# Transposing a feed-forward weight into SBUF in two parts, half of it into a buffer of its own, ahead of the end of attention

## The reference

```
x = hidden_states                       # (4, 4096, 1024) f32
# attention block
h = layernorm(x);  q, k, v = h@Wq+bq, h@Wk+bk, h@Wv+bv      # 8 heads of 128
scores = einsum('bngh,bmgh->bnmg', q, k) / 32
probs  = softmax(scores, axis=-1)       # over the 8 HEADS, for each pair of tokens
x = x + einsum('bnmg,bmgh->bngh', probs, v)
# feed-forward block
h = layernorm(x);  prev = h shifted by one token (zeros first)
xr = mu_r*h + (1-mu_r)*prev;  xk = mu_k*h + (1-mu_k)*prev
x = x + sigmoid(xr @ W_r.T) * (square(relu(xk @ W_k.T)) @ W_v.T)
```

## Time and profile before

| | us |
|---|---|
| timed runs | 1914.25 and 1846.76, median 1880.5 |
| profiled execution, whole | 1842.97 |
| its span, slowest core (core 2) | 1841.4 |
| spans of the 8 cores | 1832.2 to 1841.4 |
| TensorE, VectorE, ScalarE busy on core 2 | 1202.3, 1161.5, 949.2 |
| attention ends, last products L576 on core 2 | about 1565 |
| feed-forward, first L797 to the end of the span | 1590.05 to 1841.4 |

### The profile page before, as it was taken

One profiled execution on the slowest core, in us unless ns is written; L12 is line 12 of the kernel. 1 busy time (PEld: TensorE's weight loads), 2 busy tenths in 40 slices (PEclk: granted clock), 3 DMA queues, 4 the chain that ended last, 5 costly groups with the idle time before them and its releaser, 6 DMA issues.

```text
span 1841.4 us, 33138 instructions; the slowest of 8 cores (1832.2 to 1841.4 us)
## 1 busy us (share of the span) xinstructions
PE 1202.3 (65%) x9912; PEld 837.1 (45%) x9912; DVE 1161.5 (63%) x1864; ACT 949.2 (52%) x1216; POOL 107.2 (6%) x136
## 2 busy tenths in 40 slices
PE   1676278888884556556555665665655566468898
PEld 1443134444342555444544545454554555335554
DVE  1655022222221887888888888888888887657875
ACT  0333022222222787787878878788787866112121
POOL 1002000000000000000000000000000000000000
PEclk6676689999997998999999999899999977689999
DMA  9027933333315465464545546446454555531011
GB/s 232 5 29 89 133 42 76 76 75 76 76 59 161 123 177 148 141 190 137 155 150 165 155 141 191 140 141 176 153 155 139 169 191 170 92 69 47 24 47 58
DMA packets 157112, 219.57 MB, mean 119 GB/s; under 512 B 54032, under 2 KB 127888, under 8 KB 154704
## 3 DMA queue, kind: packets, MB, share of 16 engines
q1 hardware_dynamic: 108624, 120.98, 24.2%
q0 software_dynamic: 48320, 96.48, 21.0%
HBM read 197.51 MB, written 36.44 MB: 127 GB/s over the span
## 4 chain that ended last, share of the span: by engine, by line
PE 33%; ACT 23%; DVE 22%; DMA 10%; issue 8%; SPq 1%; DVEq 1%; ACTq 1%; POOL 0%; POOLq 0%
ACT arena L500 20%; PE stAB L226 14%; PE stAB L480 11%; DMA vtspill<-scratch 6%; DVE arena L548 5%; DVE scratch L513 3%; PE ctxP L264 2%; DMA x_res<-x 2%; DVE scratch L518 2%; DVE scratch_f L521 2%; PE stAB L797 2%; DMA arena<-qspill 1%; PE stAB L836 1%; PE ctxP L203 1%; PE stAB L857 1%
## 5 line engine op out<-in xcount | busy, mean ns | idle before, releaser
L500 ACT ACTIVATE arena<-stAB 128x2048 bf16<-128x2048 f32 (+1 forms) x288 | 513.3, 1782 | 102.2 <-PE stAB L480 94.8
L480 PE MATMUL stAB<-arena 128*128 128x256 bf16 (+1 forms) x2304 | 312.1, 282 | 372.9 <-ACT arena L500 354.8
L480 PEld LDWEIGHTS stAB<-arena 128*128 128x128 bf16 x2304 | 206.6, 102 | 449.4 <-issue 419.7
L548 DVE TENSOR_TENSOR arena<-arena,scratch 128x2048 bf16<-128x2048 bf16 (+1 forms) x288 | 335.8, 1166 | 32.8 <-PE ctxP L576 2.1
L576 PE MATMUL ctxP<-arena 128*128 128x128 bf16 x4352 | 316.1, 229 | 31.7 <-DVE arena L548 23.3
L226 PE MATMUL stAB<-arena,wa 128*128 128x512 bf16 (+1 forms) x1344 | 321.6, 398 | 11.9 <-ACT arena L337 11.9
L576 PEld LDWEIGHTS ctxP<-arena 128*128 128x128 bf16 x4352 | 285.8, 103 | 53.8 <-issue 47.5
L513 DVE TENSOR_TENSOR scratch<-arena 128x1024 bf16<-128x1024 bf16 (+1 forms) x288 | 190.8, 663 | 85.2 <-ACT arena L500 68.7
L226 PEld LDWEIGHTS stAB<-arena,wa 128*128 128x128 bf16 x1344 | 136.4, 103 | 173.3 <-issue 51.9
L253 DVE TENSOR_SCALAR scratch<-scratch,cvecsb 128x512 bf16<-128x512 bf16 (+1 forms) x104 | 36.6, 352 | 253.5 <-ACT scratch L249 253.5
L249 ACT ACTIVATE scratch<-stAB 128x512 bf16<-128x512 f32 (+1 forms) x104 | 59.2, 572 | 252.5 <-PE stAB L226 183.3
(11 more groups left out here) (60 smaller groups left out, 785.9 us busy)
## 6 DMA issues: line engine op xcount, KB each, us to landing
arena<-kspill SPq DMA_DIRECT2D x72, 1024.0 KB, 9.2
arena<-vtspill POOLq DMA_DIRECT2D x72, 1024.0 KB, 10.6
x_res<-x SPq DMA_DIRECT2D x1, 8704.0 KB, 35.3
kspill<-scratch SPq DMA_DIRECT2D x8, 1024.0 KB, 5.3
vtspill<-scratch SPq DMA_DIRECT2D x8, 1024.0 KB, 9.2
out<-x_res SPq DMA_DIRECT2D x8, 1024.0 KB, 4.1
qspill<-scratch SPq DMA_DIRECT2D x8, 544.0 KB, 2.8
arena<-qspill POOLq DMA_DIRECT2D x8, 512.0 KB, 12.3
```

The source lines that it names most:

```text
L480: r = e.matmul(stAB[:, g * w:(g + 1) * w], arena_ap(KQ0 + par_k * 4096 + g * 512 + mcq * 128, [[1, 128]]), arena_ap(qbase2 + g * w, [[1, w]]),
L500: return e.activation(arena_ap(EA0 + par_e * 2048, [[1, NH * w]]), stAB[:, 0:NH * w], AF.Exp, scale=1.0 / 32.0)
L548: lambda e, w=w, par_u=par_u, par_e=par_e, par_d=par_d: e.tensor_tensor(arena_ap(UB0 + par_u * 2048, [[1, NH * w]]), arena_ap(EA0 + par_e ...
```

## The change

W_k's eight transposes leave the loop of 24. Four of them (`cj` 4 to 7) go to a new SBUF buffer `wkbuf` (4096 bfloat16 columns, 8 KB on each partition) and wait only for `d_ws0`; in SP's order they stand behind attention's last k load. The other four (`cj` 0 to 3) go where they went before, columns 8192 to 12287, which is the v buffer of the even quads, and wait for the products of step 283 (`m_ctx[NIT - 5]`), the last that reads that buffer. The order of `cj` in the queue becomes 4, 5, 6, 7, 0, 1, 2, 3. The sixteen transposes of W_r and W_v keep gates and order. The L797 matmuls read `cj` 4 to 7 from `wkbuf`; their number and order stay.

```diff
     ctxs = sbuf("ctxs", 2048, F32)
+    wkbuf = sbuf("wkbuf", 4096, BF16)
     wa = sbuf("wa", 6144, BF16)
@@
-    for wi, gate in [(1, None), (0, ("t_ffn", 1)), (2, ("t_ffn", 9))]:
+    for cj in range(4, NC):
+        ev("sync", [("d_ws0", 16 * 12)], "d_tw",
+           lambda e, cj=cj: e.dma_start_transpose(
+               bass.AP(wkbuf, (cj - 4) * 1024, [[wkbuf.shape[1], 128], [1, 1024]]),
+               bass.AP(wspill, 8 * 128 * D + cj * 128, [[D, 1024], [1, 128]])), 16)
+    for cj in range(4):
+        ev("sync", [("t_ctx", m_ctx[NIT - 5]), ("d_ws0", 16 * 12)], "d_tw",
+           lambda e, cj=cj: e.dma_start_transpose(
+               arena_ap(8192 + cj * 1024, [[1, 1024]]),
+               bass.AP(wspill, 8 * 128 * D + cj * 128, [[D, 1024], [1, 128]])), 16)
+    for wi, gate in [(0, ("t_ffn", 1)), (2, ("t_ffn", 9))]:
         for cj in range(NC):
             gw = [("t_ctx", total_ctx), ("v_du", total_du), ("t_st", total_st),
-                  ("d_ws0", 16 * 12)]
-            if gate is not None:
-                gw.append(gate)
+                  ("d_ws0", 16 * 12), gate]
@@ op_k
-                    r = e.matmul(ps[:, 0:wch],
-                                 arena_ap((8 + cj) * 1024 + dj * 128, [[1, 128]]),
+                    if cj < 4:
+                        wsrc2 = arena_ap((8 + cj) * 1024 + dj * 128, [[1, 128]])
+                    else:
+                        wsrc2 = bass.AP(wkbuf, (cj - 4) * 1024 + dj * 128,
+                                        [[wkbuf.shape[1], 128], [1, 128]])
+                    r = e.matmul(ps[:, 0:wch], wsrc2,
```

## The result

The changed kernel took 1.0054 of the time of the kernel before (95% interval 1.004 to 1.0067): 10.0 us more on 1846.3. Its median over 13 runs was 1858.56 us (1852.82 to 1927.89), that of the kernel before over the 10 runs beside it 1846.27 us (1842.44 to 1914.25). That is inside the 2% and inside the range of 1835 to 1885, but it is a slowdown clear of the interval, and the forecast was 0.2 us.

The account below looks back on a forecast made before the run. Attention was read as bound by ScalarE's exponential, the stretch to L836 by gate `t_ffn` >= 1 and SP's issue. Terms 0 + 0.2 = +0.2 us gave 1843.2; half way to 1846.76 + 0.2 gave 1845, range 1835 to 1885.

Parts of the forecast that it names:

- Term: 0, because none was there: After attention, 1565 to 1580: moving W_k's transposes away removes no wait, since W_k already landed 9.2 us before use.
- The gates of W_r and W_v keep their waits: Feed-forward: SP reaches the gates about 12 us earlier; L836 and L857 still wait 7.0 and 12.5 us; term 0.
- The order on SP and in time: End of attention: four transposes issue behind the last k load, 1540.6 to about 1546.6; the other four from about 1559.0.
- V of quad 6 lands 1.25 us later: End of attention, step 280: v lands at 1551.45 beside the transposes, 0.2 us past its reader.
- a factor of 1.33: Slowdown assumed for v beside the transposes, from v beside the k load, 8.9 us, against v alone, 6.7.
- quad 7 "Term: 0": Last v load, read at step 284: at most 1.2 us of slowing against 2.3 us to spare, so no cost.
- The slack of 1.0 us: Step 280: v of quad 6 landed at 1550.2 and its first reader ran at 1551.21.
- The bound of 5.9 us, and 2 more for quad 7: End of attention: most that quad 6's v is delayed if served behind all four transposes, plus 2 us for quad 7's.
- If the engines take turns by packet ... 0.4 us.: Argument against a late v: its 280 packets let only about 280 short transpose packets pass, 0.4 us.
- The slower rival: Attention's tail, product of step 280, waits for v: up to 6.9 us, 1850; chance 0.2.
- The faster rivals: Feed-forward starts when W_k is there, gain 0, or W_r issues sooner, at most 7.0 us, 1836; chance 0.05.

Follow-up runs that it names:

- x5_own_sems: Kernel before, W_k, W_r and W_v each on their own semaphore and the t_ffn gates removed: 0.9883 of the kernel before.
- x3_plain256: Changed kernel with the four early transposes replaced by plain DMAs of the same bytes in 256-byte pieces: 1.0024 of the kernel before.
- x4_one_early: Changed kernel with one of the four wkbuf transposes early and the other three behind attention's end: 1.0041 of the kernel before.
- x2_after_v: Changed kernel with the four early transposes also waiting until quad 7's v load has landed: 1.0006 of the kernel before.
- p1_probe: Changed kernel, its early transposes replaced by one transpose per quad of slices 2 to 5, in four positions: spans 1896 to 1923 us, before some 1840.
- y3_iso_sp: Kernel before plus an unread 1 MB load from SP, ahead of W_k's eight transposes at attention's end: load landed in 6.6 to 8.5 us.
- y2_iso_pool: Kernel before plus an unread 1 MB load from GpSimd beside W_k's eight transposes at attention's end: load landed in 7.2 to 8.4 us.

## Why the prediction was right in part and wrong in its number

- *"Term: 0, because none was there", for W_k's leaving the stretch from 1565 to 1580.* Right: from attention's end to the end of the span it is 277.0 us after, 277.3 before; in the changed kernel's core 2 the first L811 waited 12.85 us for the mix, as before.
- *The gates of W_r and W_v keep their waits.* Right: 5.9 and 11.1 us. x5_own_sems shows that this was where the time lay.
- *The order on SP and in time.* The distances between k, the first transpose and v are right to 0.1 us (0.6 and 0.6 against 0.6 and 0.7). The length of the issue is not: 24.75 us for four, not 6, so that the other four began at 1565.29 and not at 1559.0. That cost nothing, as W_k still landed over 20 us before L811.
- *V of quad 6 lands 1.25 us later, "a factor of 1.33", quad 7 "Term: 0".* This is the step that failed. V of quad 6 landed 10.8 us later on core 2 (19.7 against 8.9), v of quad 7 14.8 us later (21.5 against 6.7), and the L577 products waited 10.6 to 19.1 us over the eight cores (median 13.2) in place of 0 to 1.8. The place was right, the size was short by a factor of about nine. The slack of 1.0 us was right for core 2 alone: on five of the eight cores the kernel before already waited for v there. I took the price of a neighbour from k beside v, two plain loads, as it was the only pair in the trace. x3_plain256, the plain form of the same bytes, came out between (12.6 us); the transposing form did not.
- *The bound of 5.9 us, and 2 more for quad 7.* Wrong as a bound. It added up packet times measured alone: four transposes at 5.9 us of all engines. In company their packets took about 79 ns in the mean where they took 22 alone, as some stood for up to 3.3 us. A bound of this sort holds only if the cost of a packet stays what it was.
- *"If the engines take turns by packet ... 0.4 us."* Refuted by x4_one_early: one transpose, about 1056 packets, held v up by as much as 11 us.
- *The slower rival*, chance 0.2, 1850: the right mechanism in the right place, under-priced. Its sign, a wait for v of over 1 us near the end, is what came. It gave 6.9 us at the most where 10 were lost. By the rule of the Trainium skill that I set beside the row (DMA: Bandwidth & Descriptors, Issuing engines are not separate DMA queues), the DMAs interleave; the runs agree so far that the streams hold each other up, but the rule tells nothing of how much: the same transfers took 1.0054 in two queues and 1.0009 in one queue and another order. The figure of the Trainium skill for a transposing DMA, 261 GB/s (DMA: Bandwidth & Descriptors, Latency and other measured facts), is not reached even alone, 2.10 MB from 1565 to 1581 being 131 GB/s; in company the issue of 1 MB alone took 24 us and more.
- *The faster rivals.* Nothing of them was seen, as their own rows said.

The forecast within 2% was right since it rested on what could be gained or lost in all; the bound behind it was wrong, and the place within the range of 1835 to 1885 owes more to the width of that range than to the sum. The 10 us were lost with one term, v beside the transposes, for which the trace held no row of its kind.

## What to carry to other kernels

A DMA that no one waits for gains nothing by going earlier, and what it costs is decided by what is in flight where it goes. Ask of each moved transfer which loads with a microsecond of slack it will lie beside; put it behind them with a wait (x2_after_v, no loss) or in a stage without tight loads. When a transfer is late, look first at why its issue is gated: a semaphore shared by several weights, with the gates that it needed, cost 21.6 us here, and a semaphore for each gave them back. A wait on an in-order queue holds up all that stands behind it: in p1_probe two such waits ahead of a k load cost 69 to 83 us.

## What the runs showed of the hardware that I had not expected

- A 256 KB transposing DMA lands in about 4 us alone. Right behind one 1 MB load on its own queue, or with one on GpSimd's queue issued 0.3 us after it, it took 6.8 to 8.7 us (y3_iso_sp, y2_iso_pool). Behind a 1 MB load on its own queue and with another on GpSimd's it took 15.4 us in the median of p1_probe's position 0 and up to 23.5, and the GpSimd load up to 22.4. With four of them all eight cores were slow (v of quad 6 in 18.7 to 21.9 us).
- In that company some packets stand for long and most do not: of the short packets of the transposes half took 18 ns, alone and in company, but 696 of 3834 took over 100 ns in place of 100 of 8192. The same bytes as plain 256-byte pieces had none over 100 ns (x3_plain256).
- The slowness has two levels rather than a slope: with one transpose v of quad 6 took 10 to 12 us on two cores and 14 to 22 on the other six, under the same program. In the 72 cores with one transpose or in isolation a k load of 8.5 us or more went with it in 21 of 26 cases.
- Behind such loads SP's issue of a transpose takes up to 13.8 us in place of 1.2 (p1_probe, core 1), so that every later DMA of SP's queue is issued later. Here no DMA with a near reader stood behind, and in p1_probe TensorE did not wait for the k load that came next (no wait for k in slices 2 to 5 outside position 3).
